# Folding the squares of a routed weight piece three times on GpSimd before the column norms

## The reference

```
x = x + attention(layernorm(x))                # x is 2 x 1024 x 512
h = layernorm(x).reshape(2048, 512)
scores = softmax(h @ gate_w)                   # 8 experts
topk_w, topk_idx = top_k(scores, 2)
g = silu(h @ w_gate[e]) * (h @ w_up[e])        # 512 x 352 per expert
routed = sum over the two experts of topk_w * (g @ w_down[e])
shared = (silu(h @ sw_gate) * (h @ sw_up)) @ sw_down
out = x + routed + shared
```

## Time and profile before

| | us |
|---|---|
| median of three runs | 685.24 |
| lowest and highest | 683.01, 685.58 |
| the profiled execution | 684.72 |
| its span, from the first to the last instruction | 683.0 |
| PE busy in the span | 648.0 |
| DVE busy | 422.7 |
| ACT busy | 266.7 |
| POOL busy | 237.6 |

### The profile page before, as it was taken

How to read it: one execution, slowest core, us unless ns; L and a number is a source line. 1 busy time by engine, 2 the same in 40 slices (tenths; PEclk the granted TensorE clock), 3 DMA queues, 4 the chain that set the end, 5 groups by cost and what they waited for, 6 DMA issues and landing times.

```text
span 683.0 us, 11791 instructions
## 1 busy us (share of the span) xinstructions
PE 648.0 (95%) x3797; PEld 427.3 (63%) x3798; DVE 422.7 (62%) x746; ACT 266.7 (39%) x397; POOL 237.6 (35%) x274
## 2 busy tenths in 40 slices
PE   7989999999999999999998999999999999999991
PEld 7767677677777756665655656666666666665560
DVE  7798987997998755867778876533333333333221
ACT  5363643464453445566665764311111111111110
POOL 6320131231103236343544352144444444443331
PEclk9999999999999999999999999999999999999997
DMA  6840013513426698596684526489777878798852
GB/s 232 314 126 16 15 48 77 163 47 85 124 63 199 185 229 188 154 183 170 161 190 144 62 42 87 63 148 131 138 131 130 136 136 130 136 136 131 115 83 41
DMA packets 110388, 86.89 MB, mean 127 GB/s; under 512 B 79280, under 2 KB 85424, under 8 KB 110352
## 3 DMA queue, kind: packets, MB, share of 16 engines
q1 hardware_dynamic: 88848, 43.94, 28.5%
q0 software_dynamic: 12864, 29.50, 25.1%
q10 hardware_dynamic: 8640, 12.98, 6.0%
HBM read 44.45 MB, written 23.33 MB: 99 GB/s over the span
## 4 chain that ended last, share of the span: by engine, by line
PE 55%; DMA 8%; DVE 7%; issue 3%; POOL 2%; SPq 2%; ACT 1%; POOLq 0%; ACTq 0%; DVEq 0%
PE ps_y L528 15%; PE ps_g L528 14%; PE ps_u L528 14%; PE ring L391 8%; DMA x_in<-x_job 3%; DMA out_dram<-y_job,job_tok 3%; PE turn_h L548 3%; DVE routed L1469 1%; DMA x_job<-xn_scratch,job_tok 1%; PE ps_norm L403 1%; SPq L764 1%; DMA out_dram<-x 1%; DVE den L1348 0%; POOL squares L989 0%; DVE col_max L1448 0%
## 5 line engine op out<-in xcount | busy, mean ns | idle before, releaser
L1134 ACT CAST hidT<-turn_h 128x384 f16<-128x384 f32 x71 | 33.9, 478 | 174.8 <-PE turn_h L548 173.7
L982 POOL DMA_INDIRECT out_dram<-y_job,job_tok x39 | 61.9, 1586 | 96.4 <-DVE y_job L1754 73.0
L528 PE MATMUL ps_g<-routed,x_in 128*128 x468 | 82.6, 313 | 2.0 <-DMA x_in<-x_job 2.0
L528 PE MATMUL ps_y<-routed,hidT 128*128 x351 | 82.1, 379 | 1.3 <-DVE hidT L1409 1.3
L391 PE MATMUL ring<-xnT_h,wq_h 128*128 128x512 f32 x192 | 78.8, 411 | 4.6 <-DVE xnT_l L1287 2.0
L391 PE MATMUL ring<-xnT_h,wq_l 128*128 128x512 f32 x192 | 76.6, 399 | 0.0
L391 PE MATMUL ring<-xnT_l,wq_h 128*128 128x512 f32 x192 | 76.5, 398 | 0.0
L528 PE MATMUL ps_u<-routed,x_in 128*128 x468 | 76.2, 313 | 0.0
L1416 DVE SCALAR_TENSOR_TENSOR hid<-ps_u,job_hid,silu 128x352 f32<-128x352 f32 x39 | 22.7, 583 | 85.5 <-PE ps_u L528 85.5
L989 POOL TENSOR_TENSOR squares<-squares 128x704 bf16<-128x704 bf16 (+1 forms) x24 | 44.6, 1858 | 84.7 <-ACT squares L1098 84.7
L889 POOL TENSOR_SCALAR var_eps<-mean_var 128x1 f32<-128x1 f32 x32 | 11.9, 371 | 171.5 <-DVE mean_var L1395 94.8
(11 more groups left out here) (236 smaller groups left out, 1102.3 us busy)
## 6 DMA issues: line engine op xcount, KB each, us to landing
x_res<-in_L_attn_x_dram SPq DMA_DIRECT2D x18, 256.0 KB, 3.6
routed<-in_L_ffn_w_gate_dram ACTq DMA_DIRECT2D x6, 704.0 KB, 4.7
routed<-in_L_ffn_w_up_dram ACTq DMA_DIRECT2D x6, 704.0 KB, 6.6
out_dram<-x SPq DMA_DIRECT2D x16, 256.0 KB, 3.4
xn_scratch<-xn_hl SPq DMA_DIRECT2D x16, 256.0 KB, 2.7
out_dram<-y_job POOLq DMA_DIRECT2D x16, 256.0 KB
x_in<-in_L_attn_x_dram SPq DMA_DIRECT2D x14, 256.0 KB, 2.7
routed<-in_L_ffn_w_down_dram ACTq DMA_DIRECT2D x6, 512.0 KB, 7.1
```

The lines of the kernel that those rows point to most:

```text
L528: ins = pe.matmul(ps, a[i][:, k, :], w(j, k), start=(start and q == 0), stop=(stop and q == len(steps) - 1))
L982: pool.indirect_dma_start(out[:, :], bass.IndirectOffsetOnAxis(job_tok[:, r:r + 1], 0), y_job[:, b, :], None, compute_op=ALU.add).then_inc ...
L1134: act.copy(hidT[:, 0], turn_h[:, 0:FC, :]).then_inc(s["hidTh_s"], 1)
```

## The change

For a routed piece POOL's `fold` adds halves three times in place of once: 704, 352 and 176 columns of a gate or up piece, 768, 384 and 192 of a down piece. The second and the third addition wait for the one before through the new semaphore `fold_in`; `fold_s` is raised by the third. PE then sums one eighth of the piece's columns with a single matmul, which starts and ends its accumulation, and DVE takes the maximum over that eighth. The shared pieces keep DVE's single fold and the two matmuls.

```
         def norms_of(m):
-            n = pieces[m][3].shape[1] // 4
-            return ps_gate[:, P:P + n] if m < SHARED_PIECES else ps_norm[:, 0:n]
+            n = pieces[m][3].shape[1]
+            return ps_gate[:, P:P + n // 4] if m < SHARED_PIECES else ps_norm[:, 0:n // 8]
...
                 pe.wait_ge(s["fold_s"], m + 1)
                 if m:
                     pe.wait_ge(s["max_s"], m)
+                if m >= SHARED_PIECES:
+                    pe.matmul(norms_of(m), ones_h[:, :], squares[:, 0:w.shape[1] // 8], start=True, stop=True)\
+                        .then_inc(s["norm_mm"], 1)
+                    return
                 n = w.shape[1] // 4
...
             def fold(m):
-                half = pieces[m][3].shape[1] // 2
                 pool.wait_ge(s["square_s"], m + 1)
-                pool.tensor_tensor(squares[:, 0:half], squares[:, 0:half], squares[:, half:2 * half], ALU.add)\
-                    .then_inc(s["fold_s"], 1)
+                for i in range(3):
+                    half = pieces[m][3].shape[1] >> (i + 1)
+                    if i:
+                        pool.wait_ge(s["fold_in"], 2 * (m - SHARED_PIECES) + i)
+                    pool.tensor_tensor(squares[:, 0:half], squares[:, 0:half], squares[:, half:2 * half], ALU.add)\
+                        .then_inc(s["fold_s" if i == 2 else "fold_in"], 1)
```

More of the change, by code:

```diff
@@ L250, in preln_decay_attention_moe @@
             gw_h_s gw_l_s gate_mm logit_s x2_out0 x2_out1 xn2_out0 xn2_out1 pad_out cst_a cst_b shared_g shared_u shared_d
-            over_0 w0 w1 w2 w3 w4 w5 w6 w7 square_s fold_s norm_mm max_s set_s upper_s split_s
+            over_0 w0 w1 w2 w3 w4 w5 w6 w7 square_s fold_s fold_in norm_mm max_s set_s upper_s split_s
             d_set d_route rt_exp rt_exp_in picked_s hot_s route_mm tables_s xin0 xin1 gin0
```

## The result

The changed kernel takes 695.84 us (median of five runs, 692.28 to 701.78) against 685.58 of the kernel before (five runs, 683.01 to 689.92). The ratio is 1.0144, with a 95% interval of 1.0104 to 1.0184: slower by 1.4%, some 10 us. Forecast were 689.3 us and a range up to 693.2.

What follows compares the result with a forecast made beforehand. TensorE was taken to set the pace. TensorE waits 5.6, DVE waits 2.4 and GpSimd held 0.9, less 4.6 saved, gave +4.3 us on 684.72: 689.0, given as 689.3 us, range 684.8 to 693.2.

Steps and rivals of the forecast that it cites:

- TensorE's saving: One short norm matmul instead of two saves 0.22 or 0.24 us in each of 20 pieces, 4.6 us.
- the four tight folds: Pieces 0, 5, 11 and 16 have at most 0.22 us between fold and norm, so longer folds delay TensorE there.
- GpSimd and DVE excluding each other: On their shared port pair, one engine's instruction holds the other's; seen at L1448 in piece 7.
- the turns they take in piece 7: Whoever waits is let in next, so the DVE chain meets two more holders, of 0.78 and 0.41 us.
- the two terms for the holds between DVE and GpSimd: DVE held by later additions, 2.4 us, and GpSimd held by DVE, 0.9 us.
- Waits of TensorE: Later fold ends make TensorE wait at pieces 0, 5, 11 and 16: 1.39, 1.28, 1.26 and 1.7, sum 5.6 us.
- The straight line: Fold time linear in columns, 2.08 ns each plus 0.05 us fixed, giving later gate or up additions 0.78 and 0.41 us.
- Waits of DVE: Later additions hold DVE's chain to hidT: 0.65 us at pieces 7, 13 and 15, 0.45 at 21, sum 2.4 us.
- GpSimd held by DVE: DVE's split delays the second addition in piece 19, 0.5 us; pieces 9 and 18 together 0.4; sum 0.9 us.
- The likely case: The forecast itself: 689.3 us, own range 687.5 to 691, folds ending 1.39 or 1.48 us later; chance 0.5.
- rival (4): Later additions stop DVE for their whole time (+2.4) and cost 0.2 us more each (+2.2): 693.9 us; chance 0.15.

Runs made afterwards that it cites:

- delay_alone: Kernel before, with eight one-column GpSimd memsets between each fold and TensorE's release; stage 160.48 us (+4.5), ratio 1.0069.
- load_alone: Kernel before, plus the second and third additions on a tile of their own, behind the fold that releases TensorE; stage 160.97 us (+5.0), ratio 1.0078.
- saving_alone: Kernel before with its single fold, but one matmul and DVE's maximum over an eighth of the columns, the rest left out; stage 152.12 us (-3.8), ratio 0.9951.
- awake_twice: Changed kernel with dummy matmuls before the norm of piece 16 and before the down product behind piece 21's norm; stage 163.36 us, ratio to kernel before 1.0125.
- awake: Changed kernel with 50 dummy matmuls before the norm of piece 16; stage 165.10 us, ratio to kernel before 1.0114.
- both: Kernel before, plus later additions on a tile of their own, the third releasing TensorE, which keeps two matmuls; stage 170.76 us (+14.8), ratio 1.0213.
- late_norm: Changed kernel with each piece's norm matmul moved behind the down product of its unit; stage 172.94 us, ratio to kernel before 1.0270.
- two_adds: Changed kernel with two additions in place of three and one matmul over a quarter of the columns; stage 161.73 us, ratio to kernel before 1.0124.
- after: The changed kernel itself, in its profile; stage 165.06 us against 155.95 for the kernel before, ratio 1.0144.
- load_memset: Kernel before, plus two memsets of 0.85 and 0.5 us on a separate tile behind each fold, in place of later additions; stage 159.95 us (+4.0), ratio 1.0071.

## Why the prediction was wrong

**Right: what kind of thing happens, and where.** TensorE's saving of 0.22 and 0.24 us a piece; the four tight folds 0, 5, 11 and 16 (delay_alone); GpSimd and DVE excluding each other (load_alone) and the turns they take in piece 7 (the rows of L1456 to L1461). The Trainium skill, SBUF — State Buffer, section "Who interferes with whom", says that a DVE instruction with two SBUF inputs contends with a GpSimd instruction that reads SBUF and not with one that only writes, while one in a 2-port mode contends with both. The trace agrees: `y_scale` 0.52 us beside an addition and 0.16 beside a memset; L1462, one input, 0.89 beside a memset. The page lists `tensor_scalar` among the instructions that can enter such a mode; that L1462 did, no run here shows apart.

**Wrong: the size, 9.1 us in place of 4.3.** Two steps failed most: the clock was put at nothing (1.7 us), and the two terms for the holds between DVE and GpSimd, 3.3 us together, measured 5.9. By the steps of the sum:

- *Waits of TensorE*, 5.6 us: measured 1.50, 1.46 (pieces 4 and 5), 1.15 and 1.86, with the saving of each put back: 6.0. Nearly right. The later additions were mis-sized: 0.85 and 0.52 us, not 0.78 and 0.41. The straight line through 704 and 768 columns gave a fixed part of 0.05 us; between 352 and 176 columns it is 0.19 (0.52 less 176 x 1.88 ns). The tight down pieces 8 and 14 lost their last tenth by it, 0.1 us in all.
- *Waits of DVE*, 2.4 us: pieces 7, 13, 15 and 21 cost 3.5 (0.95, 0.94, 0.91, 0.70). The hold itself is 0.72 in load_alone, near the 0.65. The other 0.2 at 7, 13 and 15 is TensorE's saving of the piece in front, given back here (saving_alone); 21 has none of it. I had left out of the saving the four pieces themselves, but what is lost there is the gain made in front of them.
- *GpSimd held by DVE*, 0.9 us: pieces 9, 10, 18 and 19 cost 0.49, 0.20, 0.76 and 0.92 with the saving put back, 2.4 us. Here the order of turns was wrong too. In piece 19 the fold was to come first, then the split, then the second addition. In the changed kernel the split began 0.26 us ahead of the fold, and the fold itself was held: 2.79 us in place of 1.51, while the later additions took their usual 0.85 and 0.52. The second addition is held in piece 9 (2.11 us in place of 0.85) and the third in piece 10 (1.91 in place of 0.52), also by a split (rows below). In piece 18 it is `hidT` that is late, not the fold: the fold and its additions hold L1461, `y_scale` and the split of DVE (1.39, 0.52 and 2.16 us). load_alone and delay_alone show pieces 9, 18 and 19 at 0 each, and load_alone has 0.73 at piece 17, where awake has only the saving (-0.24). So which piece pays depends on who starts first there, and only both parts together give these places: **both** has 0.24, 0.53 and 1.10 at 9, 18 and 19.
- *Not in the sum at all*: the clock, 1.7 us (awake_twice). Neither the sum nor a rival asked what a longer idle stretch of TensorE does to the work behind it.

DVE and GpSimd in piece 19, then the second addition of piece 9 and the third of piece 10:

```profile
397.46 1.68 DVE L1477 SCALAR_TENSOR_TENSOR routed<-routed,scale 128x1408 f16<-128x1408 f32 x1
397.72 2.79 POOL L997 TENSOR_TENSOR squares<-squares 128x704 bf16<-128x704 bf16 x1 [2.62 <-ACT squares L1106]
...
326.59 2.11 POOL L997 TENSOR_TENSOR squares<-squares 128x352 bf16<-128x352 bf16 x1
...
333.62 1.91 POOL L997 TENSOR_TENSOR squares<-squares 128x176 bf16<-128x176 bf16 x1
```

6.0 + 0.1 + 3.5 + 2.4 + 1.7 - 4.6 = 9.1. Of the 4.8 us beyond the forecast, the missing clock term is 1.7, the hold of GpSimd by DVE 1.5, that of DVE by GpSimd 1.1 and the tight folds 0.5. A slip of addition counts for little: 689.0 and 0.5 are 689.5, not 689.3. The likely case and rival (4) were both short: (4) came near in time (693.9), which is luck, for its reasons did not hold. DVE is not stopped for the whole of each addition (0.72 us of 1.37), a fold grew by 0.14 us more than the likely case had it and not by 0.4, and the clock is missing there as well.

Open is why the clock fell behind waits of 2.1 us (awake, late_norm) and 2.6 us (two_adds, late_norm), and did not behind one of 2.1 us (changed kernel, piece 21), 2.9 us (delay_alone) and 3.65 us (late_norm). The length of the last wait alone doesn't decide it.

## What to carry to other kernels

Work handed to an idle engine is free only where its result has time to spare: list for each instance the distance between the result and its use, and then what else that engine holds up while it is busy, here DVE's small instructions and its splits. A saving on the pacing engine counts only up to the next wait of that engine; where that wait is for a third engine, the saving is returned. And price an added idle stretch of TensorE twice, as itself and as a possible stretch at half clock behind it.

## What the runs showed of the hardware that was not expected

- TensorE's granted clock fell to 0.50, its lower level, for 3 us and more behind single waits of 2.1 to 3.5 us in a kernel in which it was busy for 92% of the span. Each time the piece behind lost 1.1 to 1.7 us (after, awake, both, two_adds). Behind other waits of 2.1, 2.9 and 3.65 us it stayed at 1.00. With one gap filled the fall came at a later one (piece 22 in place of piece 17).
- GpSimd's addition of two bf16 tiles: 0.52, 0.55, 0.85, 0.91, 1.51 and 1.64 us for 176, 192, 352, 384, 704 and 768 columns. That is 1.9 ns a column between 176 and 352, and 2.0 to 2.1 between 704 and 768.
- A GpSimd memset holds DVE instructions of three columns for its whole duration (0.89 us, load_memset, piece 7), and lets a split of 1536 columns with two inputs run beside it undisturbed (1.82 us).
